# Seeding the mixer's output banks with the residual by ScalarE copies instead of TensorE identity products

## The chip, the cores and the metric

The kernel runs on one core of one Trainium2 chip. The time is the device time of one execution in microseconds (us), the median of several runs. The profile is of one further execution; its times count from the start of its span.

## The reference

Two sublayers work on x (4 batch rows of 1024 tokens with 128 features), both modulated from a condition c. The first is a state-space mixer, the second a mixture of eight experts with top-1 routing. What touches the change is the end of the mixer:

```python
y = y * z
y = y @ out_w.T + out_b
return jnp.clip(y + residual, -10.0, 10.0)
...
x = x + ga * _L0_attn_ref(h, ...)
h = _layernorm(x, axis=-1) * (1 + cb) + sb
x = x + gb * _L0_ffn_ref(h, ...)
```

Here `residual` is the modulated row h, and z is the gate. Of the second sublayer the mixer's stage already computes the normalized rows, the projection `x @ W_proj` and the router's logits, which decide the expert of each token.

## The kernel before, in words

Every engine has its own program, written out by hand, and engines meet only at semaphores. Nothing is scheduled automatically: an engine works through its list in order, and a wait at the head of the list holds all that is behind it. The program has four stages: the modulated and normalized rows of x; the state-space convolution as Toeplitz products; the stage of the change, which finishes the mixer and projects its rows; then the routing (one-hots, counts, places) and the 39 expert tiles. The last stage gathers rows from DRAM and scatters results back.

The stage of the change works in eight units. Unit q is half q % 2 of batch row q // 2, four tiles of 128 tokens, and its tiles fill one PSUM bank of 128x512. Units of the same half share banks: the output product of unit q is in bank 2 + q % 2, so that unit q + 2 can only begin in that bank when unit q has been read from it.

What each engine does for a unit q:

- TensorE: `gated_turn` transposes the gated rows Z (L1481). `gated_out` first writes the residual rows Hh, which already hold the bias out_b, into the bank by a product with the identity (L1489, float32, one matmul that the chip runs as two passes), and then adds the four output products (L1493). `rows_turn2` transposes the normalized rows (L1503). `project` writes the bias rows (L1514) and the projections with the router's columns (L1521). The loop over q runs `gated_turn(q + 1)`, `gated_out(q)`, `project(q - 3)` and `rows_turn2(q - 2)`; at q = 2 three filler products (L1348) stand between, and in the last iterations the order is a little different.
- ScalarE: `gated` copies the transposed gated rows to SBUF (L797), `normed` writes the normalized rows (L726, four instructions), `projected` copies the logits (L802) and the projected rows (L803), `turned2` copies the transposed normalized rows (L808). Its loop over q runs `gated(q + 1)`, `normed(q - 2)`, `projected(q - 3)` and `turned2(q - 2)`.
- VectorE: `mixer_step(q)` clips the bank (L1098), multiplies it with the gate ga (L1100) and adds it into X (L1102), which increments `s_x1`. Then come the statistics of the new rows (L927, L934) and two small operations (L1111, L1112).
- GpSimd: the reciprocal root of the variance (L619), the shift `nb` (L622), and the shifted rows into Hh (L627) for the DMAs of SyncE that put the rows into DRAM.

After unit 7 VectorE begins the routing with `assign(0)` (L1133 first), which needs the logits of units 0 to 5. Units 5 and 7 project into the banks 2 and 3 and wait for X of unit 7 (L1514 there). `normed_here` normalizes unit 7 on VectorE, and `running_counts` (L1161) needs TensorE's counts. Before the stage, GpSimd added out_b to Hh (`s_hb`, L612). Later in the kernel ScalarE already fills PSUM banks by a copy, for the experts' biases (L856, `seed_hidden`).

Of the kernel before, what the change touches and what calls it, by code (L numbers as in the profile page):

```python
# [24 lines left out]
B, L, D = 4, 1024, 128  # L25
# [3 lines left out]
HT = IC // 2  # L29
# [58 lines left out]
def adaln_program(nc, x, A_log, B_param, C_param, log_dt, in_w, in_b, out_w, out_b, ln_g, ln_b,  # L88
# [7 lines left out]
    with ctx:  # L96
        def sb(name, shape, dt=FP32):
            return ctx.enter_context(nc.sbuf_tensor(name, shape, dt))

        def sem(name):  # L100
            return ctx.enter_context(nc.semaphore(name))
# [3 lines left out]
        Hh = sb("Hh", [P, B, IC, D])  # L105
# [46 lines left out]
        ident = sb("ident", [P, P])  # L152
# [65 lines left out]
        erev = sb("erev", [P, E])  # L218
        k128 = sb("k128", [P, IC])
        seg = [sb(f"seg{k}", [P, E, n]) for k, (_, n) in enumerate(RANGES)]  # L220
        cmpk = flat_w[:, 1024:1024 + E * IC].rearrange("p (e i) -> p e i", e=E)
        nte = sb("nte", [P, E])
# [46 lines left out]
        PS = ctx.enter_context(nc.psum_tensor("PS", [P, 8, 512], FP32))  # L269
# [53 lines left out]
        s_br = sem("bias_parts_in_rows")  # L323
        s_bs = sem("bias_rows_broadcast")
        s_sh = sem("hidden_bank_seeded")
        s_so = sem("out_bank_seeded")
        s_x0 = [sem(f"first_batch_row_loaded{h}") for h in range(2)]
        s_vx = sem("input_variances_ready")
# [54 lines left out]
        s_hb = sem("biased_rows_ready")  # L383
        s_x1 = sem("x1_ready")
# [288 lines left out]
        def _(act):  # L673
            a = nc.scalar
# [41 lines left out]
            def tiles(buf, b, h):  # L716
                return buf[:, bass.ds(b, 1), HT * h:HT * h + HT, :].rearrange("p a i d -> p (a i) d")

            def normed(src, b, h, before, turned, clear):

                q = 2 * b + h
                act.wait_ge(s_nb, before + q + 1)
                if clear:
                    act.wait_ge(turned, q - 1)
                for i in range(HT):
                    last = a.activation(NR[:, HT * h + i, :], tiles(src, b, h)[:, i, :], ACT.Identity,  # L726
                                        bias=nb[:, h, i:i + 1], scale=rs[:, 1, h, i:i + 1])
                last.then_inc(s_n, 1)
# [63 lines left out]
            def gated(q):  # L792
                h = q % 2
                act.wait_ge(s_tp2, q + 1)
                if q >= 2:
                    act.wait_ge(s_op, q - 1)
                a.copy(YT2[:, HT * h:HT * h + HT, :], PS[:, h, :]).then_inc(s_nt2, 1)  # L797

            def projected(q):
                act.wait_ge(s_pj, q + 1)  # L800
                src = proj_banks(q).rearrange("p k (a c) -> p (k a) c", a=2)
                a.copy(LG[:, HT * q:HT * q + HT, :], src[:, :, D:PJ]).then_inc(s_lg, 1)  # L802
                a.copy(XF[:, HT * q:HT * q + HT, :], src[:, :, 0:D]).then_inc(s_pje, 1)  # L803

            def turned2(q):
                h = q % 2
                act.wait_ge(s_tp3, q + 1)
                a.copy(NTt[:, HT * h:HT * h + HT, :], PS[:, 4 + h, :]).then_inc(s_nt3, 1)  # L808

            gated(0)  # L810
            for q in range(2 * B + LAG + 1):
                n = q - LAG
                if q + 1 < 2 * B:
                    gated(q + 1)
                if 0 <= n < 2 * B - DVE_NORMS:
                    normed(X, n // 2, n % 2, 2 * B, s_tp3, n >= 2)
                early = 2 * B - DVE_NORMS <= n < 2 * B
                if early:
                    turned2(n)
                if n >= 1:  # L820
                    projected(n - 1)
                if 0 <= n < 2 * B and not early:
                    turned2(n)
# [518 lines left out]
        def _(pe):  # L1342
            m = nc.tensor
# [11 lines left out]
            for b in range(B):  # L1355
                m.matmul(MODP[:, b].rearrange("p m d -> p (m d)"), bc(scT[:, b:b + 1], [P, P]), wmf[:, 0:2 * D],
                         start=True, stop=False, skip_group_check=True)
                m.matmul(MODP[:, b, 1, :], ones3[0:1, :], ones3[0:1, :], start=False, stop=True,
                         skip_group_check=True).then_inc(s_mod, 1)
# [3 lines left out]
            for k, col in enumerate((2, 5)):  # L1363
                for b in range(B):
                    last = m.matmul(PS[:, 2 + k, b * D:b * D + D], bc(scT[:, b:b + 1], [P, P]), wm[:, col, :],
                                    start=True, stop=True)
# [8 lines left out]
                     skip_group_check=True).then_inc(s_rp, 1)  # L1375
# [35 lines left out]
            with nc.tensor.Fori(1, B) as b:  # L1411
                for h in range(2):
# [6 lines left out]
                     stop=True).then_inc(s_r2, 1)  # L1419
# [18 lines left out]
            for g in range(QD):  # L1438
                for j in range(JQ):
                    d = QD * j + g  # L1440
                    last = m.matmul(PS[QD * j:QD * j + QD, 6 + g // 16, g % 16 * QD:g % 16 * QD + QD],  # L1441
                                    Wst[:, d * NS:d * NS + QD], Um[:, :, d], start=True, stop=True,
                                    skip_group_check=True)
# [39 lines left out]

            def gated_out(q):
                h = q % 2
                if q >= 2:
                    pe.wait_ge(s_x1, q - 1)
                pe.wait_ge(s_hb, q // 2 + 1)
                m.matmul(PS[:, 2 + h, :], ident[:], Hh[:, q // 2, HT * h:HT * h + HT].rearrange("p i d -> p (i d)"),  # L1489
                         start=True, stop=False, skip_group_check=True)  # L1490
                pe.wait_ge(s_nt2, q + 1)
                for i in range(HT):
                    last = m.matmul(PS[:, 2 + h, P * i:P * i + P], YT2[:, HT * h + i, :], outwT[:],  # L1493
                                    start=False, stop=True, skip_group_check=True)
                last.then_inc(s_op, 1)
# [46 lines left out]
            for q in range(2 * B + LAG + 1):  # L1542
                n = q - LAG
                if q + 1 < 2 * B:
                    gated_turn(q + 1)
                if q < 2 * B:
                    gated_out(q)
                if n == 0:
                    fill(6, MOD[:, 0].rearrange("p b d -> p (b d)"), 3)
                early = 2 * B - DVE_NORMS <= n < 2 * B  # L1550
                if n >= 1 and early:
                    project(n - 1)
                if n == 2 * B - 1:
                    counts(0)
                if early:
                    rows_turn2(n)
                    fill(4, MOD[:, 0].rearrange("p b d -> p (b d)"), 1)
                if n >= 1 and not early:
                    project(n - 1)
                if 0 <= n < 2 * B and not early:  # L1560
                    rows_turn2(n)
# [6 lines left out]
            for t in range(NT):  # L1568
# [5 lines left out]
                elif t % OHC == 0:  # L1574
                    pe.wait_ge(s_oh, min(t // OHC, ACT_OHC) + 1)
                last = m.matmul(PS[:, 5, 0:3 * MAX_TILES], OR[:, t, :], OT[:, t].rearrange("p c g -> p (c g)"),
                                start=(t == 0), stop=(t == NT - 1))
# [112 lines left out]
```

## Time and profile before

| | us |
|---|---|
| median of 3 runs | 286.89 |
| lowest and highest | 285.7 and 287.5 |
| profiled execution | 286.6 |
| its span | 284.8 |
| TensorE busy | 238.7 |
| VectorE busy | 217.4 |
| ScalarE busy | 187.7 |
| GpSimd busy | 164.8 |

The span runs from the first to the last instruction; the profiled execution's own time holds 1.8 us around it. Busy time is that of the instructions themselves, without waiting. The output stage of the mixer lies between about 86 and 125 us. The rest of the kernel is the same in both versions.

### The profile page before, as it was taken

The numbers are of one execution on the slowest core, as the hardware profiler recorded it, in microseconds if no ns is written. First come the engines' busy times: TensorE is split into PE (matmuls) and PEld (weight loads), VectorE is DVE, ScalarE is ACT, GpSimd is POOL, SyncE is SP. The second block draws the span as 40 slices with busy tenths as digits, with TensorE's granted clock in tenths as the row PEclk, the third lists the DMA queues.
The fourth block names the chain that finished last, engine by engine and source line by source line (L and its number), as shares of the span: only waits on it lengthen the run. The fifth ranks groups of instructions, "written<-read, shape, count | busy, mean of one in ns | idle before, by whom it ended". The sixth has DMA issues, their size and how long they took to land.

```text
span 284.8 us, 6510 instructions
## 1 busy us (share of the span) xinstructions
PE 238.7 (84%) x1683; PEld 163.8 (58%) x1684; DVE 217.4 (76%) x893; ACT 187.7 (66%) x492; POOL 164.8 (58%) x203
## 2 busy tenths in 40 slices
PE   0998899979989999899876999979899799987630
PEld 0564655578967687654423776646566466655430
DVE  7889996988845999899544687778888687789730
ACT  3669757598613677759315689768887688778520
POOL 6669764000570666510453578878887878886760
PEclk9999999999999999999999899999999999999985
DMA  5940179951929899999142222222323222221000
GB/s 146 247 148 1 31 189 271 288 165 27 238 50 340 241 292 298 285 285 383 52 128 56 66 67 81 77 67 74 92 88 92 85 70 78 74 75 50 28 5 0
DMA packets 47603, 37.94 MB, mean 133 GB/s; under 512 B 4614, under 2 KB 42621, under 8 KB 47322
## 3 DMA queue, kind: packets, MB, share of 16 engines
q1 hardware_dynamic: 42600, 27.33, 34.0%
q0 software_dynamic: 3744, 9.77, 11.8%
q10 hardware_dynamic: 1234, 0.53, 0.8%
q8 instruction: 12, 0.20, 0.3%
q14 instruction: 13, 0.11, 0.1%
HBM read 26.96 MB, written 11.08 MB: 134 GB/s over the span
## 4 chain that ended last, share of the span: by engine, by line
PE 33%; POOL 29%; issue 11%; DVE 10%; DMA 5%; ACT 4%; SPq 4%; POOLq 0%; ACTq 0%; DVEq 0%
POOL out_dram L650 9%; POOL rs L661 6%; POOL SBk L641 5%; PE PS L1597 5%; POOL BIG L641 4%; PE PS L1348 3%; PE PS L1618 3%; DMA BIG<-k_pad 3%; PE PS L1493 3%; PE PS L1489 2%; PE PS L1521 2%; DMA X<-in_L_attn_x_dram 2%; POOL rs L569 2%; PE PS L1428 2%; PE PS L1441 2%
## 5 line engine op out<-in xcount | busy, mean ns | idle before, releaser
L867 ACT ACTIVATE V<-PS,gb1T 128x128 f32<-128x128 f32 x156 | 58.7, 457 | 6.4 <-PE PS L1609 6.0
L1597 PE MATMUL PS<-BIG,V 128*128 x78 | 43.7, 642 | 12.4 <-ACT PS L856 5.3
L1618 PEld LDWEIGHTS PS<-BIG,V 128*128 128x128 f32 x312 | 42.9, 193 | 14.6 <-issue 12.4
L1618 PE MATMUL PS<-BIG,V 128*128 x312 | 48.8, 297 | 0.9 <-ACT V L867 0.9
L650 POOL DMA_INDIRECT out_dram<-Wst,idsi x39 | 39.4, 1011 | 12.3 <-issue 10.9
L1276 DVE TENSOR_SCALAR V<-PS,mv,rs 128x512 f32<-128x512 f32 x39 | 31.2, 801 | 15.2 <-POOL rs L661 15.0
L641 POOL DMA_INDIRECT SBk<-rows,idgi x27 | 28.4, 1051 | 21.8 <-DVE idsi L1236 15.2
L1253 DVE BATCH_NORM_STATS2 st<-PS 128x6 f32<-128x512 f32 x39 | 27.0, 692 | 9.4 <-PE PS L1597 4.9
L856 ACT COPY PS<-Z 128x512 f32 x36 | 21.3, 591 | 15.0 <-DVE V L1276 9.8
L661 POOL TENSOR_TENSOR rs<-ve,half 128x4 f32<-128x4 f32 (+3 forms) x25 | 22.7, 907 | 14.4 <-DVE ve L1297 14.1
L1609 PE MATMUL PS<-ident,V 128*128 128x128 f32 x156 | 24.5, 280 | 5.1 <-DVE V L1276 3.1
L1597 PEld LDWEIGHTS PS<-BIG,V 128*128 128x128 f32 x78 | 11.6, 188 | 21.1 <-issue 21.0
L612 POOL TENSOR_TENSOR Hh<-Hh,outb 128x1024 f32<-128x1024 f32 x4 | 9.5, 2414 | 24.2 <-ACT SBk L771 24.2
L1609 PEld LDWEIGHTS PS<-ident,V 128*128 128x128 f32 x156 | 17.9, 143 | 7.4 <-DVE V L1276 5.2
L850 ACT COPY V<-PS 128x128 f32<-128x128 f32 x39 | 10.7, 274 | 12.3 <-PE PS L1584 12.3
L619 POOL TENSOR_TENSOR rs<-ve,half 128x4 f32<-128x4 f32 x8 | 8.1, 1018 | 17.7 <-DVE ve L1112 16.5
L1348 PE MATMUL PS<-MOD,ident 128*128 128x512 f32 x40 | 18.1, 594 | 0.0
L569 POOL TENSOR_TENSOR rs<-ve,half 128x4 f32<-128x4 f32 x16 | 16.6, 1039 | 1.3
L1263 DVE BATCH_NORM_STATS2 st<-PS 128x6 f32<-128x128 f32 x39 | 11.1, 284 | 8.0 <-PE PS L1621 4.8
L726 ACT ACTIVATE NR<-Hh,nb,rs 128x128 f32 (+1 forms) x32 | 13.2, 481 | 6.0 <-DVE nb L939 6.0
L1398 PE MATMUL PS<-inwG,NTt 128*128 128x256 f32 x64 | 15.3, 382 | 0.9 <-ACT NTt L732 0.9
L1398 PEld LDWEIGHTS PS<-inwG,NTt 128*128 128x128 f32 x64 | 12.0, 190 | 6.6 <-ACT NTt L732 3.4
(263 smaller groups left out, 520.6 us busy)
## 6 DMA issues: line engine op xcount, KB each, us to landing
BIG<-k_pad SPq DMA_DIRECT2D x32, 256.0 KB, 5.6
BIG<-in_L_ffn_W_dram SPq DMA_DIRECT2D x1, 2048.0 KB, 9.5
rows<-GL SPq DMA_DIRECT2D x4, 512.0 KB, 4.5
rows<-Hh SPq DMA_DIRECT2D x8, 256.0 KB, 4.5
out_dram<-Hh SPq DMA_DIRECT2D x8, 256.0 KB, 4.5
rows<-U SPq DMA_DIRECT2D x4, 512.0 KB, 4.1
Z<-in_L_ffn_b_dram SPq DMA_DIRECT2D x1, 2048.0 KB, 9.1
X<-in_L_attn_x_dram SPq DMA_DIRECT2D x3, 512.0 KB, 6.4
```

The lines of the kernel that those rows point to most:

```text
L569: g.tensor_tensor(rs[:, w, h, :], ve[:, w, h, :], half[:, 0:HT], ALU.pow).then_inc(done, 1)
L641: pool.indirect_dma_start(out=XG[u], out_offset=None, in_=rows, in_offset=bass.IndirectOffsetOnAxis(ap=idgi[:, t:t + 1], axis=0), bounds_c ...
L650: pool.indirect_dma_start(out=out_rows, out_offset=bass.IndirectOffsetOnAxis(ap=idsi[:, t:t + 1], axis=0), in_=FO[:, t % FRING, :], in_off ...
L661: g.tensor_tensor(rs1[:, at, cols], ve1[:, at, cols], half[:, cols], ALU.pow).then_inc(s_rsd1, 1)
L867: a.activation(AT[:, u, k, :], PS[:, 3, P * k:P * k + P], ACT.Gelu, bias=gb1T[:, 1, bass.ds(e, 1), k], scale=gb1T[:, 0, bass.ds(e, 1), k]) ...
L1253: return step.mark(v.bn_stats(st1[:, t % RING, 0, :], PS[:, t % RING, :]))
L1276: v.tensor_scalar(NH[:, t % RING, :], PS[:, t % RING, :], mv1[:, at, col, 0:1], rs1[:, at, col:col + 1], ALU.subtract, ALU.mult).then_inc( ...
L1348: m.matmul(PS[:, bank, :], ident[:], rows, start=True, stop=True)
L1398: last = m.matmul(dst, NTt[:, HT * h + i, :], inwG[:], start=False, stop=True, skip_group_check=True)
L1597: last = m.matmul(PS[:, u, :], XT[:, u, :], W1s[:, bass.ds(e, 1), :].rearrange("p a h -> p (a h)"), start=not seeded, stop=seeded, skip_gr ...
L1609: last = m.transpose(PS[:, 3, P * k:P * k + P], NH[:, u, P * k:P * k + P], ident[:])
L1618: last = m.matmul(dst, AT[:, u, k, :], W2s[:, bass.ds(e, 1), k, :].rearrange("p a d -> p (a d)"), start=(first and k == 0), stop=(not firs ...
```

## The change

From unit 2 on, ScalarE copies the residual rows into the bank, and TensorE waits for that copy instead of writing them itself; the output products add to them as before. The copy for unit q + 2 stands in iteration q of ScalarE's loop, between `normed` and `projected`, and takes over TensorE's wait for `s_x1` (X of unit q is written). Units 0 and 1 keep the identity product.

```diff
+        s_sm = sem("mixer_bank_seeded")
...
+            def seed_rows(q):
+
+                act.wait_ge(s_x1, q - 1)
+                act.wait_ge(s_hb, q // 2 + 1)
+                a.copy(PS[:, 2 + q % 2, :],
+                       Hh[:, q // 2, HT * (q % 2):HT * (q % 2) + HT].rearrange("p i d -> p (i d)")).then_inc(s_sm, 1)
...
                 if 0 <= n < 2 * B - DVE_NORMS:
                     normed(X, n // 2, n % 2, 2 * B, s_tp3, n >= 2)
+                if q + 2 < 2 * B:
+                    seed_rows(q + 2)
...
             def gated_out(q):
                 h = q % 2
-                if q >= 2:
-                    pe.wait_ge(s_x1, q - 1)
-                pe.wait_ge(s_hb, q // 2 + 1)
-                m.matmul(PS[:, 2 + h, :], ident[:], Hh[:, q // 2, HT * h:HT * h + HT].rearrange("p i d -> p (i d)"),
-                         start=True, stop=False, skip_group_check=True)
+                if q < 2:
+                    pe.wait_ge(s_hb, q // 2 + 1)
+                    m.matmul(PS[:, 2 + h, :], ident[:],
+                             Hh[:, q // 2, HT * h:HT * h + HT].rearrange("p i d -> p (i d)"),
+                             start=True, stop=False, skip_group_check=True)
+                else:
+                    pe.wait_ge(s_sm, q - 1)
                 pe.wait_ge(s_nt2, q + 1)
```

The order of ScalarE's instructions at the start of the stage, before the change, from the gated copies of units 0 to 3 (V is the gated rows' buffer) to the turned rows of unit 0:

```order
L797 COPY V<-PS 128x512 x4
L726 ACTIVATE NR<-X,nb,rs 128x128 x4
L808 COPY NTt<-PS 128x512
L797 COPY V<-PS 128x512
L726 ACTIVATE NR<-X,nb,rs 128x128 x4
```

And with the change (ten lines of new code move L797 to L798, L726 to L727 and L808 to L809); L815 is the new copy:

```order
L798 COPY V<-PS 128x512 x2
L815 COPY PS<-Hh 128x512
L798 COPY V<-PS 128x512
L815 COPY PS<-Hh 128x512
L798 COPY V<-PS 128x512
L727 ACTIVATE NR<-X,nb,rs 128x128 x4
L815 COPY PS<-Hh 128x512
L809 COPY NTt<-PS 128x512
L798 COPY V<-PS 128x512
L727 ACTIVATE NR<-X,nb,rs 128x128 x4
```

The copy for unit 2 now stands in front of the gated copy of unit 2, that for unit 3 in front of the gated copy of unit 3, and that for unit 4 in front of the turned rows of unit 0.

ScalarE in iteration 4, with what each instruction waits for, before:

```order
L726 ACTIVATE NR<-X,nb,rs 128x128 [waits norm2_rows_transposed,norm_shifts_ready]
L726 ACTIVATE NR<-X,nb,rs 128x128 x3
L802 COPY Wst<-PS 128x32 [waits projections]
L803 COPY U<-PS 128x512
L808 COPY NTt<-PS 128x512 [waits norm2_rows_transposed]
L797 COPY V<-PS 128x512 [waits out_products,gated_rows_transposed]
```

And with the change:

```order
L727 ACTIVATE NR<-X,nb,rs 128x128 [waits norm2_rows_transposed,norm_shifts_ready]
L727 ACTIVATE NR<-X,nb,rs 128x128 x3
L815 COPY PS<-Hh 128x512 [waits biased_rows_ready,x1_ready]
L803 COPY Wst<-PS 128x32 [waits projections]
L804 COPY U<-PS 128x512
L809 COPY NTt<-PS 128x512 [waits norm2_rows_transposed]
L798 COPY V<-PS 128x512 [waits out_products,gated_rows_transposed]
```

The logits, the projected rows, the turned rows and the next gated copy now come behind the new copy and its wait.

TensorE in one iteration, before:

```order
L1503 MATMUL PS<-ident,NR 128x128 x4
L1481 MATMUL PS<-ident,Z 128x128 x4
L1489 MATMUL PS<-Hh,ident 128x512
L1493 MATMUL PS<-outwT,V 128x128 x4
L1514 MATMUL PS<-part_pb,rowsel 128x2x136 x2
L1521 MATMUL PS<-WPB,NTt 128x136 x4
```

And with the change:

```order
L1515 MATMUL PS<-ident,NR 128x128 x4
L1491 MATMUL PS<-ident,Z 128x128 x4
L1505 MATMUL PS<-outwT,V 128x128 x4
L1526 MATMUL PS<-part_pb,rowsel 128x2x136 x2
L1533 MATMUL PS<-WPB,NTt 128x136 x4
```

The identity product is gone, and the order of the others is the same.

## Rows read from the trace of the kernel before

**Rows 1.** The page, part 1: busy us (share of span) and instructions.
```profile
PE 238.7 (84%) x1683; PEld 163.8 (58%) x1684; DVE 217.4 (76%) x893; ACT 187.7 (66%) x492; POOL 164.8 (58%) x203
```

**Rows 2.** Chain of waits, 70 to 150 us, shares by line.
```profile
by line: PE PS L1348 11.9%; DMA BIG<-k_pad 9.4%; PE PS L1493 8.9%; PE PS L1489 8.6%; PE PS L1521 8.5%; SPq L466 4.9%; PE PS L1481 4.4%; PE PS L1597 4.2%; PE PS L1503 3.8%; issue 2.8%; PE PS L1514 2.1%; DVE SBk L1223 2.0%; DVE SBk L1220 1.9%
```

**Rows 3.** Stretch 97 to 117 us: busy us (instructions) by engine, granted clock, DMA.
```profile
97.00:117.00 20.00, 19.86 (x135) 15.51 (x133) 18.99 (x78) 15.42 (x39) 13.69 (x18) 1.00 0.95 276
```

**Rows 4.** Timeline, VectorE: start us, us, engine, line, operation [idle before].
```profile
94.41 0.69 DVE L1102 TENSOR_TENSOR X<-PS,X 128x512 f32<-128x512 f32 x1
...
101.73 0.69 DVE L1102 TENSOR_TENSOR X<-PS,X 128x512 f32<-128x512 f32 x1
...
107.60 0.69 DVE L1098 TENSOR_SCALAR PS<-PS 128x512 f32<-128x512 f32 x1
...
109.06 0.69 DVE L1102 TENSOR_TENSOR X<-PS,X 128x512 f32<-128x512 f32 x1
...
116.48 0.69 DVE L1102 TENSOR_TENSOR X<-PS,X 128x512 f32<-128x512 f32 x1
```

**Rows 5.** Timeline, TensorE: one unit, 104.4 to 108.7 us.
```profile
104.44 0.60 PE L1503 MATMUL PS<-ident,NR 128*128 128x128 f32 x4
104.88 0.60 PE L1481 MATMUL PS<-ident,Z 128*128 128x128 f32 x4
105.32 1.02 PE L1489 MATMUL PS<-Hh,ident 128*128 128x512 f32 x2
106.18 1.05 PE L1493 MATMUL PS<-outwT,V 128*128 128x128 f32 x8
...
107.50 1.19 PE L1521 MATMUL PS<-WPB,NTt 128*128 128x136 f32 x8
108.53 0.60 PE L1503 MATMUL PS<-ident,NR 128*128 128x128 f32 x4
```

**Rows 6.** Timeline, ScalarE: one unit, 104.6 to 108.8 us.
```profile
104.64 0.19 ACT L802 COPY Wst<-PS 128x32 f32<-128x32 f32 x1 [0.90 <-PE PS L1521]
104.73 0.59 ACT L803 COPY U<-PS 128x512 f32<-128x512 f32 x1
105.20 0.60 ACT L808 COPY NTt<-PS 128x512 f32<-128x512 f32 x1
105.68 0.62 ACT L797 COPY V<-PS 128x512 f32<-128x512 f32 x1
106.16 1.66 ACT L726 ACTIVATE NR<-X,nb,rs 128x128 f32<-128x128 f32 x4
108.73 0.19 ACT L802 COPY Wst<-PS 128x32 f32<-128x32 f32 x1 [0.91 <-PE PS L1521]
```

**Rows 7.** Timeline, TensorE and VectorE behind unit 7.
```profile
117.23 0.40 PE L1514 MATMUL PS<-part_pb,rowsel 12*128 12x272 bf16 x2 [0.37 <-DVE X L1102]
...
119.26 0.35 DVE L1133 TENSOR_REDUCE top<-Wst 128x24 f32<-128x192 f32 x1 [0.44 <-ACT Wst L802]
...
122.44 0.55 DVE L1161 TENSOR_TENSOR_SCAN V<-seg,PS 128x192 f32<-128x192 f32 x1 [0.24 <-PE PS L1535]
```

**Rows 8.** Line L856, 140 to 200 us: ns min/median/max, starts.
```profile
L856 ACT COPY PS<-Z x16: 589/590/592, 149.2 to 198.5; 128x512 f32 x16
```

**Rows 9.** Timeline, TensorE: fillers at iteration 2.
```profile
93.46 2.74 PE L1348 MATMUL PS<-MOD,ident 128*128 128x512 f32 x6
```

**Rows 10.** Timeline of TensorE from 150 us, then one stretch with granted clock.
```profile
150.10 1.12 PE L1597 MATMUL PS<-BIG,V 128*128 x2 [1.39 <-ACT PS L856]
...
151.17 1.06 PE L1618 MATMUL PS<-BIG,V 128*128 x8
...
154.10 0.66 PE L1609 MATMUL PS<-ident,V 128*128 128x128 f32 x4 [1.71 <-DVE V L1276]
...
156.36 1.92 PE L1618 MATMUL PS<-BIG,V 128*128 x8
...
156.00:157.00 1.00, 1.00 (x5) 0.85 (x4) 0.61 (x1) 0.69 (x3) 0.00 (x0) 0.50 0.00 0
```

## The prediction

> **What bounds the kernel now.** I read the busy times of the page first [rows 1]. TensorE leads with 84% of the span and VectorE follows with 76%, but these are averages over stages with different limits, and they do not say what the mixer's output stage is worth. The second view is the chain of waits over 70 to 150 us [rows 2]. It puts 8.6% of these 80 us, 6.9 us, on L1489, the identity product, and reads as if all eight were on the path. The third view is the same stage by stretch [rows 3]: from 97 to 117 us TensorE is busy 19.86 of 20 us, VectorE 18.99 and ScalarE 15.42. So two engines look full, and the chain, which steps back to the previous instruction of an engine when nothing released it, stayed on TensorE. The timeline of VectorE decides it [rows 4]. Its addition into X (L1102), once a unit, starts at 94.41, 101.73 and 109.06 for units 1, 3 and 5: 7.32 and 7.33 us for two units, 3.66 each, which is the length of its own work. Only towards unit 7 (116.48) are there 7.42 us, so 0.09 us of waiting. TensorE's own unit is longer: L1503 at 104.44 and 108.53, 4.09 us [rows 5]. It began with a lead, since the first units have no projection, and spends that lead until about unit 6. VectorE therefore sets the end of the eight units, and TensorE only just fails to. ScalarE has 0.91 us of idle time in 4.09 [rows 6].
>
> **What the change removes.** Six identity products (units 2 to 7), each two passes. L1489 at 105.32 and L1493 at 106.18 [rows 5] are 0.86 us apart, so TensorE's unit falls from 4.09 to 3.23 us and TensorE does 6 x 0.86 = 5.2 us less. This is not 5.2 us of the end: VectorE's 3.66 us per unit stay. If every wait of VectorE in and just behind the stage went, it would be 0.09 us before unit 7, 0.44 before L1133 and 0.24 before L1161 [rows 4, 7], 0.77 us in all. That is the ceiling of the gain, and two of the three hang on X of unit 7 itself (TensorE's L1514 at 117.23 waits for it, then projection 5, then ScalarE's logits).
>
> **What it adds.** Six ScalarE copies of 128x512 from SBUF to PSUM. The same form stands in L856 at 590 ns [rows 8]. In a row with others a copy of that size takes 0.48 us from start to start (L808 at 105.20, L797 at 105.68, L726 at 106.16 [rows 6]). I take 0.48. The bounds are 0.09 us (the spacing of the small copy L802, 104.64 to 104.73) and 0.59 (the whole duration), plus up to 0.19 us where the second semaphore of the new wait and TensorE's weight load, until now under the identity product, come into the open; for these two I have only neighbours, the hop of 0.04 us (L1521 ends at 107.50 + 1.19 = 108.69, L802 starts at 108.73 [rows 5, 6]), and keep 0.04 a hop. The sum of spacings, 3.18 + 0.48 = 3.66 us per unit, would just fit ScalarE beside VectorE.
>
> The Trainium skill (ScalarE: Activation LUTs, "What ACT_TABLE_LOAD costs") gives a copy without pointer operands 186 ns + 0.833 ns per element with 93 ns of overlap, which would be 520 ns of spacing at 512 elements; the traced 480 ns is lower and is used. With 520 each of the four large copies in the circle below would cost 0.04 us more, 0.16 us a circle.
>
> **The new wait, and who stands behind it.** The copy for unit q+2 waits until VectorE has written X of unit q, because that frees the bank. TensorE had this wait at the last moment, in front of unit q+2. ScalarE takes it a whole iteration earlier, and behind it in its queue stand the logits and row copy of unit q-3, the turned rows of unit q-2, the gated copy of unit q+2 and the normalized rows of unit q-1. TensorE waits for the last of these (L1503) before it comes to the gated turn and the output products of unit q+2. So a circle closes over two units. From the end of X of unit q: hop 0.04, the new copy 0.48, logits 0.09, rows 0.47, turned rows 0.48, gated copy 0.48 [rows 6]; normalized rows 1.66 to their end; hop 0.04; L1503 0.44, L1481 0.44, L1493 1.05 to its end [rows 5]; hop 0.04; VectorE from L1098 at 107.60 to the end of L1102 at 109.06 + 0.69, 2.15 [rows 4]. The sum is 7.86 us, against 7.32 for two of VectorE's own units.
>
> Where it bites: for q = 0 and 1 the circle lacks TensorE's long queue, but ScalarE stands until X of unit 1 is there (94.41 + 0.69 = 95.10), and then needs 0.04 + 0.48 + 0.48 + 1.66. Normalized rows 0 end at 97.76, and TensorE, through with its fillers at 93.46 + 2.6 = 96.1 [rows 9], pauses 1.7 us. VectorE is not hurt: the output products of unit 3 still end before it needs them at 100.3. For q = 2 the circle has no logits and rows to copy, 7.86 - 0.56 = 7.30: a tie. For q = 3 it is whole: X of unit 3 ends at 101.73 + 0.69 = 102.42, that of unit 5 at 110.28 in place of 109.75, 0.53 late. Unit 6 follows at 110.28 + 3.66 and is as late. For q = 5 TensorE has no gated turn to do (there is no unit 8): 7.86 - 0.44 = 7.42, exactly what VectorE took there before [rows 4]. X of unit 7 ends at 117.70 in place of 117.17. Everything behind it (L1514, projection 5, logits, L1133) hangs on it [rows 7], and the waits in front of L1133 and L1161 stay as they are. The sum is **+0.5 us**: six copies that cost ScalarE 2.9 us, of which 2.4 lie in its idle time, and 5.2 us taken from TensorE which turn into its waiting. The profiled execution took 286.6 us (span 284.8, 1.8 around it), so 287.1; the median of the runs is 286.89, 0.3 higher, so I forecast **287.4**.
>
> With the bounds: with 0.09 for the copy the circle takes 7.47, unit 5 is 0.14 late, and at unit 7 VectorE's idle 0.09 takes back most: +0.05. With 0.59 + 0.19 it takes 8.16; the lateness adds up over both circles, 2 x 0.30 + 0.53, so +1.1, and the tie at q = 2 breaks, which makes it at most 1.4. The likeliest case has a range of its own of 286.3 to 288.6, the spread of the three runs (285.7 to 287.5) included.
>
> **Rivals.** (a) TensorE is the bound, as the chain says, and the end moves by the whole 5.2 us: 281.7. For it: 19.86 of 20 us busy. Against it: VectorE's spacing, equal to its work for six units. Even half of it would need VectorE to have idle time. 4%. (b) The copies hide entirely, because ScalarE has 0.91 us free per unit and some of VectorE's waits go: 0 to -0.4 us, 286.7. Against it: the idle time lies in front of L802, and the new wait comes before it with all the rest of ScalarE's unit behind it. 15%. (c) Slower by more than a measurement tells: TensorE's clock falls. It was granted in full from 97 to 117 us, where TensorE was idle for 0.14 of 20 us [rows 3]. The changed kernel has pauses of about 0.9 us (91.7), 1.7 us (96.1) and 0.9 us in units 3 and 4. In the trace, after a pause of 1.39 us and one of 1.71 us (before L1609 at 154.10), with 2.3 us of work between them,, the granted clock read 0.50 in the stretch 156 to 157, that is 1.2 GHz, and the 8 passes of L1618 took 1.92 us instead of 1.06 [rows 10]. At 1.8 times its time TensorE's 3.23 us become 5.8 per unit, 2.2 more than VectorE's. [...] 9%. The rest, 4%, is for what I do not see, mostly above the forecast; (d) among it, that the rows' DMAs, later by half a microsecond, hold up the first gather.
>
> The Trainium skill speaks for (c) (TensorE: Matmul & The Clock Gate, "Part 1: The HAM clock gate"): the slow clock is the default and only activity holds the fast one, so work taken from TensorE can cost clock. The trace agrees that pauses cost clock at 155 us; it does not show that pauses as thin as these do.
>
> **How the numbers follow.** Forecast 68%, (a) 4%, (b) 15%, (c) 9%, the rest 4%. A measurement of this kernel can tell about 1%, 2.9 us. Faster by over 1% is (a) and a sliver: 5%. Slower by over 1% is the upper part of (c) and some of the rest: 8%. Within 1%: 87%. The range 285.9 to 289.3 holds the forecast, (b) and the milder end of (c).
>
> **What would show it.** Right: L1102 stays 3.66 us apart through unit 4, then one gap of about 0.5 us before L1098 of unit 5; ScalarE waits for L1102 before the new copies (over 2 us before each of the first two, about 1 us before the next two); TensorE waits at L1503 for L726, 1.7 us once and about 1 us after; L1133 starts near 119.8. Wrong: L1102 closer than 3.66 us (then VectorE was no bound), gaps at VectorE from unit 3 on or over 1 us (the circle is longer), or a granted clock below 1 between 90 and 120 us.

## The result, and the profile after

| | before | after |
|---|---|---|
| median of 20 runs, us | 285.84 | 287.51 |
| lowest and highest | 284.9 and 288.41 | 285.53 and 288.87 |
| profiled execution | 286.6 (span 284.8) | 287.66 (span 285.9) |

The ratio of the times is 1.0057, with a 95% interval of 1.0035 to 1.0079: the changed kernel is slower by 1.0 to 2.3 us. The forecast was 287.4 us, a local loss of 0.5 us.

The busy times of the profiled page, part 1, which answer to [rows 1]:

```profile
PE 234.9 (82%) x1671; PEld 162.2 (57%) x1672; DVE 217.6 (76%) x893; ACT 189.9 (66%) x498; POOL 164.7 (58%) x203
```

Twelve TensorE passes fewer (1671 for 1683), six ScalarE instructions more, 3.8 us less work for TensorE, and the span is longer by 1.1 us. The same stretch as in [rows 3]:

```profile
97.00:117.00 20.00, 16.63 (x126) 14.06 (x126) 18.52 (x77) 17.66 (x43) 13.05 (x17) 1.00 0.95 277
```

TensorE fell from 19.86 to 16.63 us busy, and its clock stayed in full. ScalarE rose from 15.42 to 17.66. VectorE, which sets the end, did not rise but fell, from 18.99 to 18.52: it waits now. Its timeline shows where (columns as in [rows 4]):

```profile
90.72 0.69 DVE L1112 TENSOR_TENSOR X<-PS,X 128x512 f32<-128x512 f32 x1
...
101.71 0.69 DVE L1112 TENSOR_TENSOR X<-PS,X 128x512 f32<-128x512 f32 x1
...
108.20 0.70 DVE L1108 TENSOR_SCALAR PS<-PS 128x512 f32<-128x512 f32 x1 [0.47 <-PE PS L1505]
109.67 0.69 DVE L1112 TENSOR_TENSOR X<-PS,X 128x512 f32<-128x512 f32 x1
...
117.20 0.69 DVE L1112 TENSOR_TENSOR X<-PS,X 128x512 f32<-128x512 f32 x1
...
119.98 0.35 DVE L1143 TENSOR_REDUCE top<-Wst 128x24 f32<-128x192 f32 x1 [0.44 <-ACT Wst L803]
```

Units 0 to 3 are 3.66 us apart as before. Before unit 5 there is one large gap, on TensorE's output products; units 4, 6 and 7 come 0.07, 0.07 and 0.14 us beyond 3.66 (their X starts at 105.44, 113.40 and 117.20). From unit 3 to unit 5 the distance is 109.67 - 101.71 = 7.96 us, where [rows 4] had 7.33. X of unit 7 comes 26.48 us after X of unit 0; before it was 116.48 - 90.75 = 25.73, 0.75 us less than now. L1143 waits the same 0.44 us as before [rows 7].

ScalarE and TensorE show the circle. First ScalarE's timeline:

```profile
91.45 0.59 ACT L815 COPY PS<-Hh 128x512 f32<-128x512 f32 x1 [3.31 <-DVE X L1112]
...
95.11 0.59 ACT L815 COPY PS<-Hh 128x512 f32<-128x512 f32 x1 [2.56 <-DVE X L1112]
...
98.77 0.59 ACT L815 COPY PS<-Hh 128x512 f32<-128x512 f32 x1 [1.01 <-DVE X L1112]
...
102.43 0.59 ACT L815 COPY PS<-Hh 128x512 f32<-128x512 f32 x1 [0.54 <-DVE X L1112]
102.96 0.18 ACT L803 COPY Wst<-PS 128x32 f32<-128x32 f32 x1
...
104.47 1.66 ACT L727 ACTIVATE NR<-X,nb,rs 128x128 f32<-128x128 f32 x4
```

And TensorE's:

```profile
106.18 0.66 PE L1515 MATMUL PS<-ident,NR 128*128 128x128 f32 x4 [0.78 <-ACT NR L727]
106.67 0.60 PE L1491 MATMUL PS<-ident,Z 128*128 128x128 f32 x4
107.11 1.06 PE L1505 MATMUL PS<-outwT,V 128*128 128x128 f32 x8
```

The copy for unit 5 starts at 102.43, right behind X of unit 3 (101.71 + 0.69 = 102.40). Behind it stand the logits, the rows, the turned rows, the gated copy and the normalized rows, which end at 106.13. TensorE, idle for 0.78 us, begins L1515 at 106.18, the output products of unit 5 end at 107.11 + 1.06 = 108.17, and VectorE starts at 108.20. Every link of the wait is there, in the order of the prediction.

### The profile page after: what moved, and what is told of

The parts are those of the page before. It is cut to its first block, busy times and chain, and to the rows that moved or that the text cites. A ratio compares the mean times of both kernels' runs of the same rounds, so it can differ in the third digit from the quotient of the medians.

```text
span 285.9 us, 6498 instructions
## 1 busy us (share of the span) xinstructions
PE 234.9 (82%) x1671; PEld 162.2 (57%) x1672; DVE 217.6 (76%) x893; ACT 189.9 (66%) x498; POOL 164.7 (58%) x203
## 4 chain that ended last, share of the span: by engine, by line
PE 28%; POOL 27%; DVE 15%; issue 12%; ACT 6%; DMA 5%; SPq 4%; POOLq 0%; ACTq 0%; DVEq 0%
POOL out_dram L651 8%; POOL rs L662 6%; PE PS L1609 5%; POOL SBk L642 4%; PE PS L1630 4%; POOL BIG L642 4%; DMA BIG<-k_pad 2%; PE PS L1358 2%; DMA X<-in_L_attn_x_dram 2%; POOL rs L570 2%; PE PS L1438 2%; ACT NR L727 2%; PE PS L1408 2%; PE PS L1451 2%; PE PS L1403 2%
## 5 line engine op out<-in xcount | busy, mean ns | idle before, releaser
L1630 PEld LDWEIGHTS PS<-BIG,V 128*128 128x128 f32 x312 | 44.0, 201 | 13.9 <-issue 12.1
L1630 PE MATMUL PS<-BIG,V 128*128 x312 | 49.0, 301 | 0.9 <-ACT V L877 0.9
L642 POOL DMA_INDIRECT SBk<-rows,idgi x27 | 28.4, 1050 | 21.8 <-DVE idsi L1246 15.2
L1609 PEld LDWEIGHTS PS<-BIG,V 128*128 128x128 f32 x78 | 11.8, 190 | 21.3 <-issue 21.2
L613 POOL TENSOR_TENSOR Hh<-Hh,outb 128x1024 f32<-128x1024 f32 x4 | 9.5, 2410 | 24.5 <-ACT SBk L772 24.5
L727 ACT ACTIVATE NR<-Hh,nb,rs 128x128 f32 (+1 forms) x32 | 13.2, 482 | 7.1 <-DVE nb L949 7.1
```

The lines of the kernel that those rows point to most:

```text
L642: pool.indirect_dma_start(out=XG[u], out_offset=None, in_=rows, in_offset=bass.IndirectOffsetOnAxis(ap=idgi[:, t:t + 1], axis=0), bounds_c ...
L1609: last = m.matmul(PS[:, u, :], XT[:, u, :], W1s[:, bass.ds(e, 1), :].rearrange("p a h -> p (a h)"), start=not seeded, stop=seeded, skip_gr ...
L1630: last = m.matmul(dst, AT[:, u, k, :], W2s[:, bass.ds(e, 1), k, :].rearrange("p a d -> p (a d)"), start=(first and k == 0), stop=(not firs ...
```

## The experiments

In all of them two distances are read from VectorE's timeline: from X of unit 0 to X of unit 7, and from X of unit 0 to the first instruction of the routing. Both are free of where the stage starts, which differs between profiled executions (X of unit 0 at 90.75 before, at 89.34 in one of the experiments). The first is 25.73 and the second 28.51 us before.

**The changed kernel again.**

> The changed kernel once more, beside the kernel before, with the granted clock of every run. In its profile X of unit 7 was written 0.72 us later than before (L1112 at 117.20 against 116.48), but the medians of 20 runs lie about 1.6 us apart. Theory of the circle alone: the times differ by 0.7 to 0.8 us at equal granted clock, and the rest is how often TensorE's clock falls in the expert tiles, which differs from run to run in both kernels. Rival: the change costs a further 0.8 us in every run behind the stage; then runs of equal clock differ by 1.6 us.

Measured: X of unit 7 came 26.48 us after unit 0 (116.30 - 89.82), the routing 29.26, exactly as in the first profile. Time 1.0036 times before, interval 1.0005 to 1.0067. The spread of one kernel goes with the granted clock. A straight line through the spans and mean clocks of 95 runs of the kernel before, taken beside these experiments (the few runs over 300 us left out, here and below), gives 0.22 us less span for 0.001 more clock, and leaves 0.7 us of scatter. Set to the same clock by this line, the 12 runs of this kernel lie 0.7 us (standard error 0.2) above the 35 runs of before that were taken with them, which is the stage's 0.75. The rival's 1.6 us at equal clock is excluded. The 20 runs of the first comparison lie 1.1 us (0.1) above the line. The runs of before that belong to them have no clock on record, and the groups of runs of before lie from 0.15 us below the line to 0.5 above it, so this 1.1 is no closer figure than the 0.7.

**The copy at the end of ScalarE's iteration.**

```diff
-                if q + 2 < 2 * B:
-                    seed_rows(q + 2)
                 early = 2 * B - DVE_NORMS <= n < 2 * B
...
                 if 0 <= n < 2 * B and not early:
                     turned2(n)
+                if q + 2 < 2 * B:
+                    seed_rows(q + 2)
```

> The new copy moves to the end of ScalarE's iteration, behind the turned rows. Circle theory: the wait for X of unit q then holds back nothing that TensorE needs early, so L1112 stays 3.66 us apart for all units, X of unit 7 begins at 116.4 (0.7 earlier than in the changed kernel, 0.1 before the kernel before), and the time is 0.7 to 0.8 us below the changed kernel's, the same as before's or 0.1 less. Rival (the copies themselves, or PSUM written by ScalarE, slow the stage): unit 7 stays near 117.2.

VectorE's timeline:

```profile
90.17 0.69 DVE L1112 TENSOR_TENSOR X<-PS,X 128x512 f32<-128x512 f32 x1
...
108.51 0.69 DVE L1112 TENSOR_TENSOR X<-PS,X 128x512 f32<-128x512 f32 x1
112.38 0.69 DVE L1112 TENSOR_TENSOR X<-PS,X 128x512 f32<-128x512 f32 x1
116.04 0.69 DVE L1112 TENSOR_TENSOR X<-PS,X 128x512 f32<-128x512 f32 x1
...
118.61 0.35 DVE L1143 TENSOR_REDUCE top<-Wst 128x24 f32<-128x192 f32 x1 [0.23 <-ACT Wst L803]
```

Unit 7 is 25.87 us behind unit 0, 0.61 us better than in the changed kernel, with the same six copies and the same waits. The routing follows after 28.44 us, since the wait before it shrank from 0.44 to 0.23. Time 0.9992 times before (0.996 to 1.0023). One thing was not expected: unit 6 comes 3.87 us after unit 5, 0.21 too late, so that unit 7 is 0.14 us behind before and not 0.1 ahead. ScalarE's timeline has the reason:

```profile
107.19 1.65 ACT L727 ACTIVATE NR<-X,nb,rs 128x128 f32<-128x128 f32 x4
...
109.58 0.59 ACT L809 COPY NTt<-PS 128x512 f32<-128x512 f32 x1 [0.19 <-PE PS L1515]
110.07 0.60 ACT L815 COPY PS<-Hh 128x512 f32<-128x512 f32 x1
110.59 0.59 ACT L798 COPY V<-PS 128x512 f32<-128x512 f32 x1
111.06 1.65 ACT L727 ACTIVATE NR<-X,nb,rs 128x128 f32<-128x128 f32 x4
```

A second, shorter circle runs between ScalarE and TensorE: normalized rows 1.65, TensorE's L1515 with its two hops 0.74 (108.84 to 109.58), turned rows 0.49, the new copy 0.52, the gated copy 0.47, and then the next normalized rows, 3.87 us in all. With the copy in it this circle is longer than VectorE's 3.66, and it catches up with VectorE at unit 6. So the place of the copy in the queue costs most of what the change costs, but six copies are not free at the other place either.

**The wait without the copy.** TensorE keeps its products.

```diff
+            def seed_rows(q):
+                act.wait_ge(s_x1, q - 1)
+                act.wait_ge(s_hb, q // 2 + 1)
+                a.copy(spare[:, 4 * q:4 * q + 4], Hh[:, q // 2, 0, 0:4])
```

> TensorE keeps its identity products; ScalarE only takes the new wait at the new place, with a copy of 4 columns behind it. Circle theory: circle 7.86 - 0.48 + about 0.15 (small copy) + 0.86 (the identity product is in TensorE's part again) = 8.4 us over two units, against 7.32: units 5 and 7 are late by 1.1 us and again by 0.5 to 0.6, X of unit 7 near 118.2 to 118.8, 1.7 to 2.3 us over before. Rival (the copy is the cost, not the wait): X of unit 7 at 116.5 to 116.8.

VectorE's timeline:

```profile
89.34 0.69 DVE L1110 TENSOR_TENSOR X<-PS,X 128x512 f32<-128x512 f32 x1
...
96.67 0.69 DVE L1110 TENSOR_TENSOR X<-PS,X 128x512 f32<-128x512 f32 x1
100.35 0.69 DVE L1110 TENSOR_TENSOR X<-PS,X 128x512 f32<-128x512 f32 x1
104.50 0.69 DVE L1110 TENSOR_TENSOR X<-PS,X 128x512 f32<-128x512 f32 x1
108.76 0.69 DVE L1110 TENSOR_TENSOR X<-PS,X 128x512 f32<-128x512 f32 x1
...
116.72 0.69 DVE L1110 TENSOR_TENSOR X<-PS,X 128x512 f32<-128x512 f32 x1
```

From unit 3 to unit 5 there are 8.41 us, as the circle of 8.4 says (TensorE's identity product, which this kernel keeps, is a part of it), and from unit 2 to unit 4, where the logits and rows (0.56 us) are not in it, 7.83. Unit 7 comes after 27.38 us, 1.65 later than before, just under the expected 1.7 to 2.3; the absolute time, 116.72, cannot be held against the expected 118.2 to 118.8, because this stage began 1.4 us earlier. The time was 1.0039 times before (1.0007 to 1.0072), 1.6 us at equal clock. The wait alone costs twice what the whole change does.

**The copy without the wait.** TensorE keeps its products, and the copies go to a part of SBUF that is free at that time.

```diff
+            def seed_rows(q):
+                act.wait_ge(s_hb, q // 2 + 1)
+                a.copy(flat_s[:, 512 * (q - 1):512 * q], Hh[:, q // 2, HT * (q % 2):HT * (q % 2) + HT].rearrange("p i d -> p (i d)"))
```

> TensorE keeps its identity products; ScalarE makes the six copies at the new place, into SBUF, without waiting for X. Theory: 0.48 us fit into the 0.91 us that ScalarE has free per unit, but TensorE's lead is spent by unit 6, so that what ScalarE gives late shows a little: 0 to 0.3 us over before. Rival (the copy is the cost): 0.5 us or more at unit 7.

Measured: unit 7 after 25.73 us (115.65 - 89.92), the routing after 28.50: nothing, to 0.01 us. Time 1.0001 times before (0.997 to 1.0031). Six copies of 0.48 us in front of the logits hide in ScalarE's 0.9 us per unit. (They write SBUF here and not PSUM, and nobody waits for them.)

**No residual at all.** The rows are left out from unit 2 on.

```diff
+                if q < 2:
+                    m.matmul(PS[:, 2 + h, :], ident[:], Hh[:, q // 2, HT * h:HT * h + HT].rearrange("p i d -> p (i d)"),
+                             start=True, stop=False, skip_group_check=True)
...
-                                    start=False, stop=True, skip_group_check=True)
+                                    start=q >= 2 and i == 0, stop=True, skip_group_check=True)
```

> From unit 2 on the residual rows are left out of the mixer's output (they are neither multiplied in by TensorE nor copied by ScalarE), so the six identity products cost nothing anywhere. VectorE theory: the addition into X stays 3.66 us apart for all units; from unit 0 to unit 7 25.63 to 25.65 us, against 25.73 before, and L1133 starts 0.1 to 0.3 us earlier after unit 0 than the 28.51 us of before. Rival (TensorE is the bound): 4 to 5 us less. The stages behind route other rows than the reference, so only the stage is read.

VectorE's timeline:

```profile
89.94 0.69 DVE L1102 TENSOR_TENSOR X<-PS,X 128x512 f32<-128x512 f32 x1
...
115.58 0.69 DVE L1102 TENSOR_TENSOR X<-PS,X 128x512 f32<-128x512 f32 x1
118.10 0.35 DVE L1133 TENSOR_REDUCE top<-Wst 128x24 f32<-128x192 f32 x1 [0.19 <-ACT Wst L802]
```

25.64 us to unit 7 and 28.16 to the routing. With the 5.2 us of products gone and nothing in their place, 0.09 us is gained at unit 7 and 0.35 at the routing. A little further on, at the scan of the routing (L1161), it is 0.58 us: 121.05 - 89.94 = 31.11 us after X of unit 0, where before it was 122.44 - 90.75 = 31.69 [rows 7]. This settles what TensorE's work was worth here.

**VectorE's unit shorter.** L1111 and L1112 move to GpSimd, everything else as before.

```diff
+                step.mark(g.tensor_scalar(ve[:, 1, q % 2, :], mv[:, 1, q % 2, :, 1], LN_EPS, None, ALU.add))
+                if q < 2 * B - DVE_NORMS:
+                    step.mark(g.tensor_scalar(neg[:, q % 2, :], mv[:, 1, q % 2, :, 0], -1.0, None, ALU.mult))
+                step.settle()
                 g.tensor_tensor(rs[:, 1, q % 2, :], ve[:, 1, q % 2, :], half[:, 0:HT], ALU.pow).then_inc(s_rh, 1)
...
-                v.tensor_scalar(neg[:, h, :], mv[:, 1, h, :, 0], -1.0, None, ALU.mult)
-                v.tensor_scalar(ve[:, 1, h, :], mv[:, 1, h, :, 1], LN_EPS, None, ALU.add).then_inc(s_vh, 1)
```

> The kernel before, with VectorE's two small operations of each unit (negated mean and variance plus epsilon, L1111 and L1112) moved to GpSimd. VectorE's own unit falls by about 0.13 to 0.16 us. Theory: TensorE's 4.09 us per unit now set the end, its lead is spent by unit 5, and the addition into X of units 6 and 7 comes hardly earlier than before: 25.4 to 25.6 us from unit 0 to unit 7 instead of 25.73, L1133 at 28.3 to 28.5 after unit 0, time 0 to 0.3 us below before. Rival (VectorE is the bound with room behind it): 24.7 us.

VectorE's timeline, with its waits for TensorE:

```profile
90.47 0.69 DVE L1106 TENSOR_TENSOR X<-PS,X 128x512 f32<-128x512 f32 x1
93.86 0.69 DVE L1106 TENSOR_TENSOR X<-PS,X 128x512 f32<-128x512 f32 x1
...
107.37 0.70 DVE L1102 TENSOR_SCALAR PS<-PS 128x512 f32<-128x512 f32 x1 [0.60 <-PE PS L1494]
...
116.57 0.69 DVE L1106 TENSOR_TENSOR X<-PS,X 128x512 f32<-128x512 f32 x1
```

VectorE's unit fell by 0.28 us, to 3.38, twice what was expected, and it now waits for TensorE before each unit from unit 4 on (0.59, 0.60, 0.60 and 0.16 us); units 3 to 6 are 4.08 us apart, which is TensorE's own unit. The stage did not gain, it lost: 26.10 us to unit 7, outside the expected 25.4 to 25.6. What was forgotten is the chain through GpSimd. Its two new operations delay the shift `nb`, so ScalarE's first normalized rows begin 4.15 us after X of unit 0 (94.62 - 90.47) instead of 3.77 (94.52 - 90.75). TensorE waits 0.40 us for them at L1504, which was L1503, and everything behind is 0.38 us later, since TensorE has no further pause up to unit 7. That is the loss there (26.10 - 25.73 = 0.37). The routing, expected 28.3 to 28.5 us after unit 0, came after 28.89. Time 1.0008 times before (0.9979 to 1.0038).

**Both together, three copies.** The shorter unit, and `seed_rows` at the end of the iteration for units 5 to 7 only (`if 5 <= q + 2 < 2 * B`; TensorE keeps product and wait for units 2 to 4).

> The shorter VectorE unit of b2 together with the new copies for units 5, 6 and 7 only, at the end of ScalarE's iteration. Theory: both limits are lower, so the addition into X of unit 7 comes 24.7 to 24.9 us after unit 0 and L1133 27.6 to 27.9 us, 0.7 to 0.9 us before the kernel before; time 0.6 to 0.9 us below it. Rival (ScalarE or the waits take it back): 25.4 us or more at unit 7, no difference to b2.

VectorE's timeline:

```profile
90.62 0.69 DVE L1116 TENSOR_TENSOR X<-PS,X 128x512 f32<-128x512 f32 x1
...
115.57 0.69 DVE L1116 TENSOR_TENSOR X<-PS,X 128x512 f32<-128x512 f32 x1
```

Measured: 24.95 us to unit 7, 0.05 over what was expected, and 27.74 to the routing (118.36 - 90.62), 0.78 and 0.77 us less than before. Time 0.9952 times before, interval 0.9918 to 0.9987. With VectorE's unit shorter, TensorE's products are worth something: three copies in their place take 1.15 us off the stage of the experiment above.

**The rows left out, and the shorter unit.**

> The rows left out of the mixer's output from unit 2 on, as in b1, and VectorE's unit shorter, as in b2. Theory: VectorE is the only limit left: units 3.50 to 3.53 us apart, 24.5 to 24.7 us from unit 0 to unit 7. The floor that b3 can reach. Rival (another ring through GpSimd, whose chain is longer now): more than 24.9 us. Again only the stage is read.

VectorE's timeline:

```profile
89.80 0.69 DVE L1106 TENSOR_TENSOR X<-PS,X 128x512 f32<-128x512 f32 x1
...
113.45 0.69 DVE L1106 TENSOR_TENSOR X<-PS,X 128x512 f32<-128x512 f32 x1
...
115.98 0.35 DVE L1134 TENSOR_REDUCE top<-Wst 128x24 f32<-128x192 f32 x1 [0.45 <-ACT Wst L806]
```

23.65 us to unit 7, seven times 3.38, and 26.18 to the routing: below the expected 24.5, because the unit had become shorter than I had put in. VectorE alone would reach this (only the stage is read, since the residual is missing from the result).

**The change's place, but late units only.** `if 5 <= q + 2 < 2 * B` at the place of the change.

> The copies of the change, at their place in front of the logits, but only for units 5, 6 and 7; units 2 to 4 keep TensorE's product and its wait. ScalarE is then not held at the start of the stage, and TensorE's pauses of 0.7 to 1.4 us before unit 4 are gone. Circle theory: the circle over units 3 to 5 is whole all the same, so VectorE waits about 0.5 us before unit 5, X of unit 7 comes 26.4 to 26.5 us after unit 0, as in the changed kernel. Rival (the delay comes from the start of the stage, where ScalarE waits 3.3 and 2.6 us): 25.7 to 25.8.

VectorE's timeline, and two stretches with the granted clock (columns as in [rows 3]):

```profile
105.12 0.69 DVE L1112 TENSOR_TENSOR X<-PS,X 128x512 f32<-128x512 f32 x1
109.43 0.70 DVE L1108 TENSOR_SCALAR PS<-PS 128x512 f32<-128x512 f32 x1 [2.01 <-PE PS L1507]
```

```profile
105.00:107.00 2.00, 1.17 (x7) 1.07 (x7) 1.88 (x12) 2.00 (x7) 1.42 (x2) 0.80 1.15 347
107.00:109.00 2.00, 2.00 (x12) 2.00 (x10) 0.38 (x5) 1.80 (x6) 1.36 (x3) 0.50 1.16 345
```

The wait was 2.01 us and not 0.5. ScalarE's part had its known length: the copy started at 102.18 and the normalized rows ended at 105.88, 3.7 us as after the change. But TensorE, after pauses of 0.55 and 0.83 us with a short stretch of work between them, ran at 0.50, which is 1.2 GHz:

TensorE's timeline:

```profile
103.43 0.40 PE L1528 MATMUL PS<-part_pb,rowsel 12*128 12x272 bf16 x2 [0.55 <-ACT U L804]
...
105.94 0.90 PE L1517 MATMUL PS<-ident,NR 128*128 128x128 f32 x4 [0.83 <-ACT NR L727]
106.62 1.06 PE L1491 MATMUL PS<-ident,Z 128*128 128x128 f32 x4
107.48 1.92 PE L1507 MATMUL PS<-outwT,V 128*128 128x128 f32 x8
```

The two transposes and the products, 2.0 us after the change from L1515 to the end of L1505, took 3.5. One profile could not tell whether this kernel always does so, so it ran again.

> The kernel of c1 once more. There TensorE's clock fell to 0.50 between 105 and 109.5 us, and VectorE waited 2.01 us before unit 5 instead of 0.5. Theory: the fall is chance, the circle is not. With the clock in full through the stage, X of unit 7 comes 26.4 to 26.5 us after unit 0 and VectorE waits 0.4 to 0.6 us before unit 5; the time is 0.6 to 0.9 us over the kernel before at equal clock, more if the fall comes often. Rival (c1's kernel is slow in itself): again about 2 us before unit 5 at a full clock, and 2 us over before.

VectorE's timeline before unit 5, and the same stretch:

```profile
107.47 0.70 DVE L1108 TENSOR_SCALAR PS<-PS 128x512 f32<-128x512 f32 x1 [0.54 <-PE PS L1507]
```

```profile
105.00:107.00 2.00, 1.56 (x14) 1.56 (x15) 1.81 (x13) 2.00 (x7) 0.93 (x1) 1.00 1.15 343
```

With the clock in full the wait is 0.54 us and unit 7 comes 26.47 us after unit 0 (116.46 - 89.99), as in the changed kernel. So the circle over units 3 to 5 and 5 to 7 is the loss, and ScalarE's long waits at the start of the stage (3.31 and 2.56 us) cost nothing. The time was 1.0049 times before (1.0004 to 1.0094), 0.7 us at equal clock, as expected. Five of its 12 runs had a mean clock of 0.961 or 0.962, against two of the 17 runs of before on the same chip, and spans of 287.9 to 289.1 us. The fall in the stage may be frequent here, but that is not shown: those runs have no trace.

**All six copies, and four, with the shorter unit.**

> All six copies at the end of ScalarE's iteration, and VectorE's unit shorter as in b2. Theory: neither TensorE (3.23 us a unit) nor VectorE (3.38) is the limit now but ScalarE, 3.18 + 0.53 = 3.71 us a unit once it has no idle time left: the addition into X of unit 7 25.1 to 25.5 us after unit 0, L1133 at 27.9 to 28.2; behind b3 (24.95 and 27.74), time 0.2 to 0.6 us below before. Rival (the fewer products the better): at or below 24.7.

> As b3, with unit 4 copied by ScalarE too. Theory: VectorE's wait of 0.60 us before unit 4 in b3 shrinks to nothing, ScalarE fills up one unit earlier: unit 7 24.8 to 25.0 us after unit 0, L1133 27.6 to 27.9, the same as b3 within 0.2 us. Rival (TensorE is what is left): 0.6 us better than b3.

Six copies: 25.35 us to unit 7 (115.43 - 90.08), 28.14 to the routing, as expected for the stage. ScalarE's timeline has no idle time left but 0.19 us before the turned rows:

```profile
106.80 1.65 ACT L731 ACTIVATE NR<-X,nb,rs 128x128 f32<-128x128 f32 x4
...
109.20 0.59 ACT L813 COPY NTt<-PS 128x512 f32<-128x512 f32 x1 [0.19 <-PE PS L1516]
109.68 0.60 ACT L819 COPY PS<-Hh 128x512 f32<-128x512 f32 x1
...
110.68 1.65 ACT L731 ACTIVATE NR<-X,nb,rs 128x128 f32<-128x128 f32 x4
```

One unit of it is 110.68 - 106.80 = 3.88 us, 0.17 more than the sum of 3.71 that I had expected: it is the short circle with TensorE again, which measured 3.87 with the copy at the end alone. VectorE follows it (units 3 to 6 are 3.87 to 3.88 us apart). Time 1.0013 times before (0.9986 to 1.0039), where 0.2 to 0.6 us less was expected. Four copies: 24.87 and 27.66 us; time 0.997 (0.994 to 1.000). Three or four copies are best; they are the same within the measurement.

The stage against the whole time, for the kernels with 12 runs. The last column is the mean span over the runs of before that were taken with them, both set to the same clock by the line above, with the standard error of the difference:

| kernel | unit 0 to routing, over before | span over before at equal clock |
|---|---|---|
| changed, again | +0.75 | +0.7 (0.2) |
| copy at the end | -0.07 | -0.1 (0.2) |
| wait only | +1.66 | +1.6 (0.2) |
| copy only | -0.01 | 0.0 (0.2) |
| shorter VectorE unit | +0.38 | +0.2 (0.2) |
| shorter, three copies | -0.77 | -0.9 (0.2) |
| shorter, six copies | -0.37 | 0.0 (0.2) |
| shorter, four copies | -0.85 | -0.8 (0.2) |
| late units only, again | +0.75 | +0.7 (0.3) |

What the stage loses or gains arrives in the end, within two standard errors of each row; the six copies with the shorter unit agree least.

## Why the prediction was right

**What bounds the stage.** Right. VectorE's 3.66 us per unit held for the first four units, and with no residual work at all on TensorE (b1) they held for all eight. The chain of waits, which put 8.6% on the identity product [rows 2], was the wrong guide. With nothing in its place TensorE's saving of 5.2 us was worth 0.35 us at the routing and 0.58 at its scan, within the ceiling of 0.77. The 0.09 us of waiting that the prediction has before unit 7 lies before unit 6 (X at 109.06 and 112.82, 3.76 us apart); over the two units the sum is the same.

**The new copy.** Nearly right. It was taken at 0.48 us, and measured 0.53 to the next instruction (102.43 to 102.96). The copy itself is 0.59 us long as in [rows 8]. Copies alone, in the same place, cost nothing. What did not hold is that 3.18 + 0.48 = 3.66 us would just fit ScalarE beside VectorE: with the copy at the end of the iteration the circle of ScalarE and TensorE takes 3.87 us a unit. In the changed kernel the long circle hid this.

**The circle.** This was the forecast, and its order, place and length came out: tie for q = 2, gap before unit 5, next to none further before unit 6 (0.07 us), a small one before unit 7. It was sized 0.10 us too short, 7.96 for 7.86 from unit 3 to 5 and 117.20 - 109.67 = 7.53 for 7.42 from 5 to 7. From unit 3 to 5 half of that is the copy's 0.53. The other half is TensorE's first transposes after a pause, 0.49 us from L1515 to L1491 where [rows 5] show 0.44 in an unbroken row. At unit 7 both circles' shortfalls add up, so the sum of +0.5 us became +0.75. That step, "a copy of that size takes 0.48 us", and the 0.44 for L1503, are the terms that were mis-sized; the copy's lies inside the bounds given for it, and the 0.44 had none of its own. The tie at q = 2 left 0.07 us.

Of the signs that were named, ScalarE's waits before the new copies were 3.31, 2.56 and 1.01 us as told, but the fourth 0.54 for about 1. TensorE's long pause was 1.41 us (until 97.81) and not 1.7: the normalized rows ended at 97.76 as computed, but the fillers ran until 93.66 + 2.74 = 96.40, 0.3 later. The pauses after it were 0.69, 0.78, 0.29 and 0.79 us for about 1. The waits and pauses at the start of the stage cost VectorE nothing, as the kernel with late units only shows (26.47 us with them gone, 26.48 with them).

**The whole time.** 287.51 against 287.4, partly by luck: the forecast counted from a median of three runs, 286.89, and the median of before over 20 runs is 285.84. From there +0.5 us would have given 286.3, 1.2 us short. The difference, 1.67 us, is larger than the +0.5 forecast; the traces and the table account for about 0.75, and the other 0.9 us between the two medians is not explained.

**The rivals.** (a), TensorE as the bound, fell with b1. (b), the copies hide, is wrong at the place of the change and nearly right at another: with the copy at the end of the iteration the loss is gone but for 0.14 us at unit 7, and at the routing altogether. (c), a falling clock, did not happen in the changed kernel's trace, where the clock read 1.00 throughout the stage, but happened in its close relative c1, in just this stage. There it cost 1.5 us in one unit, where the prediction had 2.2 for a unit, in a kernel whose pauses were shorter, 0.55 and 0.83 us, than the 1.7 us that I had named. The passage at 155 us, from which the rival was drawn [rows 10], came again in the changed kernel with nearly the same pauses, 1.35 us before 150.79 and 1.72 before 154.79, and there the granted clock read 1.00 from 156 to 157 us and L1630, the same eight passes, took 1.06 us. It deserved its chance, and the length of a single pause was not the right thing to look at. What decides whether the clock falls stays open. (d), the later row DMAs, left no mark: from the first instruction of the routing to the last of its index computation it took the same in both kernels (18.76 us before, 18.77 after), and the later stage's wait of GpSimd for `idsi` is 15.2 us in both.

## What to carry to other kernels

Before moving work off a full engine, look whether another engine's instances of one line are spaced by exactly its own work: then that engine is the bound, and the first one's saving is worth only the other's idle time. When a wait moves to another in-order engine, ask what is queued behind it and whether the awaited event depends on that through a second or third engine; add up that circle and compare it with the bound's own period. The same instruction at the end of the iteration instead of the middle was 0.6 to 0.8 us cheaper, and a shift of small work off the bounding engine had to come along before TensorE's products were worth removing.

## What the runs showed that I had not expected

VectorE's two operations on 128x4 cost 0.28 us a unit, more than their own spacing in the timeline lets one think (0.08 and 0.07): from the start of the last aggregate instructions (L934) to the first instruction of the next unit the distance fell from 0.47 us (107.13 to 107.60) to 0.19 (92.22 to 92.41), so 0.13 us of settling went with them. Two circles held back this stage, and the second, between ScalarE and TensorE alone, was seen only when the first was gone. The granted clock fell to 0.50 in a stage with pauses below 1 us, once in a kernel and not in the next trace of the same kernel. And the mean clock of a run orders the times of one kernel: about 0.22 us of span for 0.001 of clock, so kernels whose times differ by less than 1 us are better compared at equal clock or by a distance inside one stage, which repeated to 0.01 us where the clock did not fall.
